# A graph-layer kernel's prologue: the degree of a tile's remaining edges by one comparison, the key sums on VectorE, and a VectorE loop of six tiles a turn

## What is computed

```python
xn = layernorm(x)
deg = segment_sum(edge_weight and 1 for the self loop, dst)     # per node
dis = where(deg > 0, rsqrt(deg), 0)
h = (layer_norm(xn) * g + b) @ W6.T                             # scaled by dis, gathered by source later
K = elu(xn @ Wk) + 1
KV = einsum('nshd,nshv->nhdv', K, xn @ Wv); Ksum = K.sum(axis=1)
```

## Time and profile before

| | us |
|---|---|
| median of three runs | 4409.62 (4406.24 to 4411.97) |
| the profiled execution | 4410.59 |
| its span, first to last instruction | 4408.9 |
| first gather on POOL | 292.45 |

### The profile page before, as it was taken

The page is one execution under the profiler, slowest core; times in us unless marked ns, Lnnn a source line. Parts: engine busy times, 40 slices in busy tenths (PEclk is TensorE's granted clock), DMA queues, the critical chain, the costliest instruction groups (busy, mean ns, idle before and its releaser), DMA issues.

```text
span 4408.9 us, 94163 instructions
## 1 busy us (share of the span) xinstructions
PE 3638.7 (83%) x26872; PEld 3080.6 (70%) x26873; DVE 2482.9 (56%) x8817; ACT 1197.3 (27%) x3161; POOL 3103.0 (70%) x3427
## 2 busy tenths in 40 slices
PE   5986676676777677777677999999999999999999
PEld 4765565565565565555556888888888888888878
DVE  7654555455454455555454665665666565665655
ACT  2430110110111110010013444444444444444434
POOL 3347777777777777777776777777777777777772
PEclk9988888887888888888888999999999999999999
DMA  4034444443444444444443343343343343333331
GB/s 147 30 117 119 129 130 123 126 130 117 127 130 125 123 130 125 124 128 127 118 127 105 114 119 112 118 119 112 114 119 114 114 119 112 119 118 116 115 110 53
DMA packets 256045, 515.37 MB, mean 117 GB/s; under 512 B 61480, under 2 KB 154032, under 8 KB 255984
## 3 DMA queue, kind: packets, MB, share of 16 engines
q0 software_dynamic: 151392, 413.60, 32.2%
q1 hardware_dynamic: 104592, 101.17, 6.9%
HBM read 474.81 MB, written 39.71 MB: 117 GB/s over the span
## 4 chain that ended last, share of the span: by engine, by line
PE 46%; DVE 14%; POOL 13%; issue 12%; DMA 7%; ACT 4%; DVEq 2%; POOLq 1%; SPq 1%; ACTq 0%
PE bank L1233 44%; POOL gs L560 12%; DMA gr<-h_d,idx_r 7%; DVE ss L989 2%; PE bank L1256 2%; DVE rstd L757 1%; DVE rstd L756 1%; ACT L736 1%; DVE rstd L755 1%; DVE st L764 1%; ACT bank L736 1%; DVE w L1130 1%; POOLq L264 1%; ACT w L739 1%; DVEq L264 1%
## 5 line engine op out<-in xcount | busy, mean ns | idle before, releaser
L560 POOL DMA_INDIRECT gs<-h_d,idx_all x3038 | 2896.4, 953 | 955.3 <-issue 654.6
L1233 PE MATMUL bank<-gs,ss 128*128 128x256 f32 x6272 | 1599.7, 402 | 10.0 <-DMA gs<-h_d,idx_all 9.6
L1233 PEld LDWEIGHTS bank<-gs,ss 128*128 128x128 f32 x6272 | 1216.9, 202 | 194.7 <-DMA gs<-h_d,idx_all 21.3
L989 DVE TENSOR_SCALAR ss<-iw,dst_f,ew 128x128 f32<-128x128 f32 x3152 | 886.0, 353 | 178.6 <-PE bank L1233 127.7
L736 ACT ACTIVATE bank<-bank,eb1c 128x128 f32<-128x128 f32 x1616 | 448.8, 341 | 634.4 <-PE bank L1233 633.8
L1233 PE MATMUL bank<-experts,w 128*128 128x256 f16 x4848 | 604.4, 278 | 16.4 <-DVE w L1130 16.2
L1233 PE MATMUL bank<-w,experts 128*128 128x128 f16 x9696 | 608.3, 219 | 0.0
L1233 PEld LDWEIGHTS bank<-w,experts 128*128 128x128 f16 x9696 | 569.1, 98 | 44.4 <-issue 16.6
L1233 PEld LDWEIGHTS bank<-experts,w 128*128 128x128 f16 x4848 | 467.6, 100 | 90.5 <-issue 21.7
L1233 PE MATMUL bank<-gr,sr 128*128 128x256 f32 x232 | 114.9, 590 | 471.2 <-DMA gr<-h_d,idx_r 471.2
L1130 DVE SCALAR_TENSOR_TENSOR w<-bank,w 128x512 f16<-128x512 f32 x404 | 277.9, 688 | 361.3 <-ACT w L739 361.1
(11 more groups left out here) (270 smaller groups left out, 3484.6 us busy)
## 6 DMA issues: line engine op xcount, KB each, us to landing
gs<-h_d,idx_all POOLq DMA_INDIRECT x3038, 2.8
hself<-h_d SPq DMA_DIRECT2D x100, 128.0 KB
ew_in<-in_eW SPq DMA_DIRECT2D x49, 168.0 KB, 2.5
out<-u SPq DMA_DIRECT2D x51, 128.0 KB
u<-xn_d SPq DMA_DIRECT2D x50, 128.0 KB, 3.0
h_d<-u SPq DMA_DIRECT2D x50, 128.0 KB, 1.9
u<-x_d SPq DMA_DIRECT2D x50, 128.0 KB
u<-r_d SPq DMA_DIRECT2D x50, 128.0 KB
```

Source lines behind the costliest of these rows:

```text
L560: pool.indirect_dma_start(gs[:, n, :], None, table[:, :], bass.IndirectOffsetOnAxis(ap=idx_all[:, w, n:n + 1], axis=0), element_offset=P * ...
L989: m = dve.tensor_scalar(ss[:, slot + j, :], iw[:, :], dst_f[:, bass.ds(c, 1)], ew[:, bass.ds(c, 1)], ALU.is_equal, ALU.mult)
L1233: return pe.matmul(out_ap, lhsT, rhs, start=first, stop=last, **kw)
```

## The change

- **Rest pass.** POOL compares a rest column's destination, in f32 and less the tile's first node, with 0 to 127 in one instruction (128 columns) into `ohr`, and copies the weight's three parts (3 columns) into `ew_r`. TensorE multiplies these into three columns of their own (`rest_bank`), which it first clears with a matmul of zeros. VectorE sums the three columns per tile into `deg_x` (next to `degrees_own`), and the roots add `deg_x` to the folded degrees: one more link on POOL, none on VectorE. Between iterations POOL waits for its own comparison.
- **Key sums.** The matmuls of K against `valid` go. VectorE adds K times `valid` to `k_sum` (the buffer `u4`), tile by tile, and four small matmuls at the end give the total over the nodes.
- **VectorE's loop** takes six tiles an iteration for two. The register load for the next tile is issued behind the node comparison; only the first of a turn stands at its head. The order in a tile is now: sum of quarters (t), quarter comparison (t+1), node comparison, weighting, keys (t), rows of h (t), key sum (t), source list (t+1), own degrees and `deg_x` (t+1). The weighting waits for the quarter comparison (`dve_deg`), no longer for the node comparison, and the sum of quarters of a tile stands a tile later.
- The closing matmul that signals `deg_ps` is bf16 for f32. Two constants fewer are set on POOL.

```diff
@@ -250,6 +251,9 @@
     return bank[4 * b][:, 0:PARTS * Q * PACK]
+def rest_bank(b):
+    return bank[4 * b][:, PARTS * Q * PACK:PARTS * Q * PACK + PARTS]
@@ -488,19 +490,14 @@
         with pool.Fori(after - 1, lo + (OWN - DEG + FRONT), 1) as c:
-            pool.tensor_tensor(own_qn, dst_qn[:, :, bass.ds(c, 1)].rearrange("p a c -> p (a c)"),
-                               tile_qn[:, bass.ds(t, 1), :].rearrange("p a c -> p (a c)"),
+            pool.wait_ge(s["deg_rest_set"], c + off + 1)
+            pool.tensor_tensor(own_r, dst_all[:, bass.ds(c, 1)], win_first[:, bass.ds(t, 1)],
                                ALU.subtract).then_inc(s["rest_own"], 1)
+            pool.wait_ge(s["deg_rest_used"], c + off + 1)
+            pool.tensor_copy(ew_r, ew_parts[:, :, bass.ds(c, 1)].rearrange("p a c -> p (a c)"))
             pool.wait_ge(s["rest_own"], c + off + 1)
-            pool.wait_ge(s["deg_rest_used"], c + off + 1)
             pool.sem_inc(s["gate"], 1)
-            pool.tensor_scalar(ohr_q, iota_qb[:, 0:Q], own_qn[:, 0:1], None, ALU.is_equal)
-            pool.tensor_scalar(ohr_node[:, :, 0], iota_nb[:, :], own_qn[:, 1:2], None,
-                               ALU.is_equal).then_inc(s["rest_hot"], 1)
-            pool.wait_ge(s["rest_hot"], c + off + 1)
-            pool.tensor_tensor(ohr_w[:, :, :, 0], ohr_q.unsqueeze(1).to_broadcast([P, PARTS, Q]),
-                               ew_parts[:, :, bass.ds(c, 1)].to_broadcast([P, PARTS, Q]),
-                               ALU.mult).then_inc(s["deg_rest_set"], 1)
+            pool.tensor_scalar(ohr, iota_p[:, :], own_r, None, ALU.is_equal).then_inc(s["deg_rest_set"], 1)
@@ -508,6 +505,7 @@
         pool.wait_ge(s["deg_out"], i + 1)
+        pc.link(pool.tensor_tensor(v, v, deg_x[:, CUTS[i]:CUTS[i + 1]], ALU.add))
         pc.link(pool.tensor_scalar(v, v, 1.0, None, ALU.add))
@@ -895,30 +893,38 @@
-    def degrees(t, b):
-        lo = own_column(dve, t)
+    def degrees_quarter(t, lo):
         cols = bass.ds(lo + (OWN - DEG + FRONT), DEG)
...
         dve.tensor_tensor(oh_q, dst_q[:, cols].unsqueeze(1).to_broadcast([P, Q, DEG]),
-                          iota_qb[:, bass.ds(t * Q, Q)].unsqueeze(2).to_broadcast([P, Q, DEG]), ALU.is_equal)
+                          iota_qb[:, bass.ds(t * Q, Q)].unsqueeze(2).to_broadcast([P, Q, DEG]),
+                          ALU.is_equal).then_inc(s["dve_deg"], 1)
+    def degrees_weighted(t, b, lo, following=None):
+        cols = bass.ds(lo + (OWN - DEG + FRONT), DEG)
         own_n = dst_n[:, cols].rearrange("p (g c) -> p g c", c=PACK)
         shape = [P, DEG // PACK, QN, PACK]
-        dve.tensor_copy(idx_all[:, bass.ds(t, 1), :].rearrange("p a c -> p (a c)"),
-                        src_row[:, bass.ds(lo, OWN)]).then_inc(s["idx_listed"], 1)
         dve.tensor_tensor(oh_node[b], iota_nc.unsqueeze(1).to_broadcast(shape), own_n.unsqueeze(2).to_broadcast(shape),
-                          ALU.is_equal).then_inc(s["dve_deg"], 1)
+                          ALU.is_equal)
+        lo_next = own_column(dve, following) if following is not None else None
         dve.wait_ge(s["dve_deg"], t + 1)
...
                           ALU.mult).then_inc(s["deg_set"], 1)
+        return lo_next
+    def index_list(t, lo):
+        dve.tensor_copy(idx_all[:, bass.ds(t, 1), :].rearrange("p a c -> p (a c)"),
+                        src_row[:, bass.ds(lo, OWN)]).then_inc(s["idx_listed"], 1)
...
         dve.tensor_tensor(deg_own[b], deg_bank(b).rearrange("p (a c) -> p a c", c=PACK),
-                          pick.unsqueeze(1).to_broadcast([P, PARTS * Q, PACK]), ALU.mult).then_inc(s["deg_read"], 1)
+                          pick.unsqueeze(1).to_broadcast([P, PARTS * Q, PACK]), ALU.mult)
+        dve.tensor_reduce(deg_x[:, bass.ds(t, 1)], rest_bank(b), AX.X, ALU.add).then_inc(s["deg_read"], 1)
@@ -931,6 +937,12 @@
                                  op1=ALU.add).then_inc(s["k_done"], 1)
+    def key_sum(t):
+        dve.wait_ge(s["k_done"], t + 1)
+        dve.wait_ge(s["k_summed"], t + 1)
+        dve.scalar_tensor_tensor(out=k_sum[:, :], in0=u1[:, :], scalar=valid[:, bass.ds(t, 1)], in1=k_sum[:, :],
+                                 op0=ALU.mult, op1=ALU.add).then_inc(s["k_summed"], 1)
@@ -940,27 +952,37 @@
     dve.wait_ge(s["pool_links"], EDGE_LINKS)
-    degrees(0, 0)
+    dve.memset(k_sum[:, :], 0.0).then_inc(s["k_summed"], 1)
+    first_lo = own_column(dve, 0)
+    degrees_quarter(0, first_lo)
+    degrees_weighted(0, 0, first_lo)
+    index_list(0, first_lo)
     degrees_own(0, 0)
-    degrees_sum(0, 0)
-    with dve.Fori(0, (W - 1) // 2) as p:
-        for b in (1, 0):
-            t = 2 * p + (1 - b)
-            degrees(t + 1, b)
+    with dve.Fori(0, (W - 1) // TURN) as p:
+        lo = own_column(dve, TURN * p + 1)
+        for j in range(TURN):
+            t, b = TURN * p + j, (j + 1) % 2
+            degrees_sum(t, 1 - b)
+            degrees_quarter(t + 1, lo)
+            lo_next = degrees_weighted(t + 1, b, lo, t + 2 if j < TURN - 1 else None)
             keys(t)
+            rows_h(t)
+            key_sum(t)
+            index_list(t + 1, lo)
             degrees_own(t + 1, b)
-            rows_h(t)
-            degrees_sum(t + 1, b)
+            lo = lo_next
+    degrees_sum(W - 1, 0)
     last_w = slice(CUTS[2], W)
...
     deg, y, mh, tmp = (v[:, last_w] for v in (deg_w, w_s1, w_s2, w_s3))
-    ch.link(dve.tensor_scalar(deg, deg, 1.0, None, ALU.add))
+    ch.link(dve.scalar_tensor_tensor(out=deg, in0=deg, scalar=1.0, in1=deg_x[:, last_w], op0=ALU.add, op1=ALU.add))
     ch.link(dve.tensor_scalar(dis[:, 1 + CUTS[2]:], deg, 0.0, None, ALU.is_gt))
...
     rows_h(W - 1)
+    key_sum(W - 1)
@@ -1274,6 +1295,7 @@
             pe.wait_ge(s["deg_read"], t - 1)
+        mm(rest_bank(b), zero_b, zero_b[:, 0:PARTS], True, True)
         for g in range(DEG // PACK):
@@ -1281,11 +1303,11 @@
         with pe.Fori(0, n, 1) as i:
-            pe.wait_ge(s["deg_rest_set"], base + i + 1)
-            mm(deg_bank(b), ohr_node.rearrange("p n c -> p (n c)"), ohr_w.rearrange("p a q c -> p (a q) c"), False, True,
+            pe.wait_ge(s["deg_rest_set"], base + i + (REST_FROM + 2))
+            mm(rest_bank(b), ohr, ew_r, False, True,
                skip_group_check=True).then_inc(s["deg_rest_used"], 1)
-        mm(bank[4 * b][0:1, D:D + 1], zero_tile[:, 0:1], zero_tile[:, 0:1], True, True).then_inc(s["deg_ps"], 1)
+        mm(bank[4 * b][0:1, D:D + 1], zero_b[:, 0:1], zero_b[:, 0:1], True, True).then_inc(s["deg_ps"], 1)
@@ -1306,10 +1328,7 @@
         for k in range(KB):
-            mm(wide(5 + k), t_b[b][:, k * P:(k + 1) * P], u1[:, :], False, True, skip_group_check=True)
-        for k in range(KB):
-            m = mm(bank[5 + k][:, D:D + 1], u1[:, k * P:(k + 1) * P], valid[:, bass.ds(t, 1)], False, True,
-                   skip_group_check=True)
+            m = mm(wide(5 + k), t_b[b][:, k * P:(k + 1) * P], u1[:, :], False, True, skip_group_check=True)
         m.then_inc(s["kv_acc"], 1)
@@ -1340,6 +1359,9 @@
     key_rows(W - 1, 0)
+    pe.wait_ge(s["k_summed"], W + 1)
+    for k in range(KB):
+        mm(key_total[:, k:k + 1], k_sum[:, k * P:(k + 1) * P], valid[:, 0:1], True, True)
     pe.wait_ge(s["kxT_set"], KB)
```

26 lines of the change are left out of this document (12 added, 14 removed).

## The result

The changed kernel takes 4389.66 us in the median of six runs (4387.88 to 4390.22), the kernel before in the same job 4411.22: a ratio of 0.9951, 95% interval 0.9938 to 0.9964. That is 21.6 us less; forecast were 4383 us and some 27 less. The profiled execution took 4389.59 us, 21.0 less than that of before.

The account below looks back on a forecast made before the run. Three near-equal limits bound the prologue loop: TensorE 3.53, VectorE 3.58, a chain about 3.5 us. 46 tiles at 3.65, plus 8.3, roots 6.2 and clock 2.0, make 184.4 against 211.7; net -26.9, 4383 us, range 4374 to 4400.

Parts of the forecast that it names:

- TensorE 3.53: Prologue tile if TensorE bounds: 3.94 us less 0.36 for the removed valid matmuls and some 0.05 of waiting.
- VectorE 3.54 in the slow form: VectorE's summed work per prologue tile with the slow node comparison: 3.54 us; 3.24 in the fast form.
- The meeting, 3.65: Prologue tile where TensorE, VectorE and a chain through exp, all near 3.5 us, meet: a little above the largest, 3.65.
- rival B: Prologue tiles: the meeting costs nothing and TensorE's shed weight loads count too; 3.48 us a tile, 4375 us; chance 0.08.
- POOL 2.9 a tile, not the bound: POOL's rest pass per prologue tile: 2.9 us, 0.7 to spare, its 128-column comparison (0.45 to 0.8) hidden under register loads.
- Roots, 3.1 lost each: Two root stages of the prologue: about 4.05 us a tile against 3.65, plus fold wait 0.9 and root's end 0.6.
- The clock dip, 2.0: Granted clock's fall in the prologue, 0.94 in the mean between 183 and 209.9 us, may come again: 2.0 us.
- Later stages unchanged within 3: Stages behind the prologue: unchanged within about 3 us, for a clock that falls elsewhere.
- A: Prologue tiles: VectorE and POOL couple through the lock on SBUF; 4.0 us a tile, 4399 us; chance 0.20.
- C: VectorE's loop: register load not hidden, as the weighting waits for the sequencer; 4.23 us a tile, 4410 us; chance 0.07.
- D: Prologue tiles: POOL's 128-column comparison holds the port against VectorE; 4.8 us a tile, 4436 us; chance 0.04.
- The rule on the shared port: VectorE instructions with two SBUF inputs and GpSimd instructions reading SBUF exclude each other; POOL's subtraction takes 1.01 us, alone 0.19.

Follow-up runs that it names:

- the first three kernels of the experiments: Changed kernel with, singly, keys' sum back on TensorE, old rest pass, register load at the tile's head; ratios to the kernel before 0.9958, 0.9968, 0.9972.
- The last run: Kernel before with one SBUF allocation 32 bytes longer, no instruction changed, against the kernel before on that chip: ratio 0.9958 (0.9943 to 0.9974).

## Why the prediction was right, and where it was off

Right was the mechanism: the tile is set by three engines within tenths of each other, work taken off all of them shortens it, and the register load hides behind the comparison. That the total came within 6 us was in part luck. The profiled execution was forecast at 4383.7 and took 4389.6. The 5.9 us come of: plain tiles -3.8 + 0.3, tile 1 to 2 -1.1, root stages +4.6 + 3.3, ahead of tile 1 -0.8 and behind tile 48 -0.85, part behind the first gather +4.3 (rounded terms). So the tiles outside the roots gave 4.6 us more than forecast, and that paid for a good half of the 7.9 that the root stages cost more. Of the prediction's own signs, 24.0 us less from the first to the last transposes came for 26 to 28, and tiles of 3.4 to 3.6 for 3.6 to 3.7.

- **TensorE 3.53**: mis-sized, 3.38. The valid matmuls were priced by the start-to-start distance, 0.36, on the ground that their weight loads "run under neighbours". They do, but they delay the group behind: 0.44 against the earlier trace rows. The run with the matmuls put back splits the way from 3.94 to 3.38: 3.82 is reached without touching them (waiting that the old stretch held, and the lighter degree group, where the forecast allowed 0.05), and 0.44 is theirs.
- **VectorE 3.54 in the slow form**: 3.38, from many terms that were each some hundredths too large (keys 0.34 for 0.40, own degrees 0.12 for 0.16, the sum 0.17 for 0.20). Key sum (0.40 to the next start) and reduction (0.30) came as forecast. The hidden load is right, and shown by undoing it; the turn's head is right in kind, 0.52 / 6 = 0.09 for 0.15.
- **The meeting, 3.65**: 3.51 in tiles 2 to 29, near rival B's 3.48: the meeting cost next to nothing. It is 3.69 in tiles 34 to 43, most of them 3.60, where ScalarE also scales rows of h and VectorE's keys wait for its exp (six times, 2.6 us). That these tiles are ScalarE's is argued from the waits alone; no run changed ScalarE.
- **Own degrees last in the tile, so that their wait goes**: right; the earlier trace rows shows 0.38 in a plain tile, the waits above only seven, 10.1 us in all, none of them in tiles 2 to 29.
- **POOL 2.9 a tile, not the bound**: right in the plain tiles (2.47 in the rows without steps above, and no wait of TensorE for it outside the root stages); its 128-column comparison takes 0.61 us, and 0.83 to 0.90 under VectorE's key sum (below), within 0.45 to 0.8 only when alone.
- **Roots, 3.1 lost each**: the step that failed. With the clock dip's share, 22.3 us were forecast for each stage, and 26.9 and 25.6 came; against plain tiles of 3.38 they lost 26.9 - 16.9 = 10.0 and 25.6 - 16.9 = 8.7. By its terms, in the first root: a tile with a step, put at 4.05 four times, took 4.26, 4.97 and, without the root's end, 4.82. The root's end, put at 0.6, took 1.25 (182.50 to 183.75): L523 takes 0.91 us in the row above, where the same operation took 0.29 before, and VectorE's node comparison starts in the same moment. The wait for the fold, "0.9 us, as now", has no row behind it; it was 3.5 and 0.3 us before and 3.0 and 4.2 now. Taking the steps out gives back 5.0 and 5.7, so their price is shown; that the stretched operations hold a good part of the rest is argued from their lengths. What is left above 16.9 without the steps, 5.0 and 3.0, goes with the fold's wait, the seed and the closing tile, and no run divides it further.
- **The clock dip, 2.0**: it came again, and a second time in the other root stage: 0.94 and 0.93 in the mean, 26.9 x 0.06 + 25.6 x 0.07 = 3.4 us against 1.6 from the earlier trace rows. Each time TensorE had stood for 2.1 to 2.2 us, waiting for POOL, shortly before the clock fell. In the second root stage the last tile, 7.47 us where it was 5.04, takes back more than the four ahead of it had gained.
- **Tail +0.4**: -0.45 (17.1 to 16.7 us from the last transposes to the first gather). The key sum there is not on the path: without any key sum it is 16.8.
- **Later stages unchanged within 3**: 4.3 more by the profiled executions, 3.7 by the medians, and not clear of the noise. TensorE's matmuls of the rest gathers (columns behind the fixed ones, gathered one by one) wait longer for their landing. Part 5 of the page, the kernel before, then the changed one:

```profile
L1233 PE MATMUL bank<-gr,sr 128*128 128x256 f32 x232 | 114.9, 590 | 471.2 <-DMA gr<-h_d,idx_r 471.2
```

```profile
L1255 PE MATMUL bank<-gr,sr 128*128 128x256 f32 x232 | 115.1, 590 | 480.4 <-DMA gr<-h_d,idx_r 480.3
```

  The same part took 4115.0, 4114.7 and 4123.2 us in the first three kernels of the experiments, with the same code in it. It does not go with the length of the prologue (276.8, 279.0 and 277.0 us to the first gather). Single executions of one kernel on that chip lie up to 7 us apart, though, so that it goes with the build is not shown either. The last run shows that a build with no instruction changed can differ by more; what did it here stays open.
- **Rivals**: A fell (3.51 us a tile outside the roots, not 4.0; POOL's operations are stretched, VectorE's are not). B had the plain tile nearly right, and its 4375 us not, as the roots took the rest. C fell, by the run with the load at the head. D fell: VectorE's node comparison has a median of 1.050 us, as in the earlier trace rows, and is never longer than 1.071 in the changed kernel.
- **The rule on the shared port** held: POOL's operations of 0.2 to 0.6 us are stretched where VectorE works with two inputs in SBUF. It was priced as a risk for plain tiles, where POOL had 0.7 us to spare and the stretch cost nothing. In the root stages POOL has nothing to spare, so there it should cost; how much, no run isolates. Source view of POOL's comparison and subtraction (ns min/median/max) in the changed kernel:

```profile
L500 POOL TENSOR_SCALAR gs<-iota_p,gs x49: 603/841/905, 53.1 to 248.4; 128x128 bf16<-128x128 f32 x49
```

```profile
L494 POOL TENSOR_TENSOR gs<-dst_all,win_first x49: 189/191/933, 52.4 to 247.2; 128x1 f32 x38, 128x1 f32<-128x1 f32 x11
```

  The comparison has only one tensor input, and is still stretched by up to 0.30 us.

## What to carry to other kernels

When engines are within tenths of each other, undoing one part says what it holds, not what it is worth: here the parts sum to 30.7 for a change worth 24.0, and work freed on all of them at once is what moves the tile. Price separately the few tiles in which an engine has extra duties, with stretched durations and with the register loads that the extra duty uncovers: here ten of 47 tiles gained nothing. Look at the granted clock of a stage before its length is compared with another run's. Read the unedited part of the span by its own length too: a build with no instruction changed moved the kernel by 27 us on one chip.

## What the runs showed of the hardware that was not expected

- A way back in VectorE's loop costs 0.52 us at two and at six tiles of code, and 3.22 us of idle (4.7 us of tile, part of it TensorE at half clock) at 24 tiles, with two packets of instructions arriving meanwhile; 48 tiles straight cost nothing.
- Two engines whose work per tile is equal (3.38 and 3.38) do not make up a lateness of 0.5: it is handed on as tiles of 3.54, which are gone when VectorE has the 0.4 us of the key sum less.
- Four f32 matmuls of one column cost TensorE 0.44 us, 0.37 of it until the next start and the rest in the group behind.
- VectorE's key sum, with two inputs in SBUF, stretches GpSimd's comparison of 128 columns from 0.61 to 0.84 us in the median.
- TensorE at a granted clock of 0.85 takes 3.80 us for the tile that takes 3.38 at 1.00.
- Lengthening one allocation in SBUF by 32 bytes changed the whole kernel by 0.42% on one chip.
